# Edge counting in a graph network kernel: TensorE's register values are loaded behind the steps of the preceding epoch, ahead of the wait for the eviction

## What is computed

```python
aggr = jax.ops.segment_sum(x[src], dst, num_segments=x.shape[0])
h = aggr @ W_rel + b_rel + x @ W_root
...
agg = jax.ops.segment_sum(h[edge_src], edge_dst, num_segments=N) * inv_deg
return h @ W_self.T + agg @ W_neigh.T + b
```

## Time and profile before

| | us |
|---|---|
| median of 3 runs | 4267.49 |
| lowest and highest run | 4263.15, 4274.33 |
| span of the profiled execution | 4266.3 |
| TensorE matmuls busy in that span | 3043.3 |
| VectorE busy | 2017.8 |
| GpSimd busy | 2364.9 |
| ScalarE busy | 705.0 |

### The profile page before, as it was taken

How to read it: one execution, slowest core, us unless ns; L and a number is a source line. 1 busy time by engine, 2 the same in 40 slices (tenths; PEclk the granted TensorE clock), 3 DMA queues, 4 the chain that set the end, 5 groups by cost and what they waited for, 6 DMA issues and landing times.

```text
span 4266.3 us, 42581 instructions
## 1 busy us (share of the span) xinstructions
PE 3043.3 (71%) x12281; PEld 2000.6 (47%) x12281; DVE 2017.8 (47%) x4124; ACT 705.0 (17%) x1923; POOL 2364.9 (55%) x2466
## 2 busy tenths in 40 slices
PE   5666798996888888888376666666667666666666
PEld 3555454554666666565243333333344333433334
DVE  7777685467988888898631111111112111111112
ACT  2334201002444444343320000000001000000000
POOL 3000000004777777776237777777775777777776
PEclk8778898998999999899675555555557555555555
DMA  3544754463444444443041111111123111111112
GB/s 125 214 191 194 302 215 190 200 263 97 119 115 114 118 110 118 110 118 97 3 149 53 53 53 53 53 53 52 53 70 142 53 53 53 52 53 53 52 53 63
DMA packets 236740, 456.14 MB, mean 107 GB/s; under 512 B 64036, under 2 KB 183570, under 8 KB 231392
## 3 DMA queue, kind: packets, MB, share of 16 engines
q1 hardware_dynamic: 158728, 291.44, 18.8%
q0 software_dynamic: 77792, 161.98, 13.9%
HBM read 336.68 MB, written 116.51 MB: 106 GB/s over the span
## 4 chain that ended last, share of the span: by engine, by line
POOL 37%; PE 26%; issue 17%; DMA 15%; DVE 4%; ACT 2%; SPq 0%; ACTq 0%; DVEq 0%; POOLq 0%
POOL edge_buffers L574 21%; POOL round_buffers L1124 16%; DMA edge_buffers<-rel_table,relidx 13%; PE sums L794 9%; PE sums L602 4%; PE sums L706 3%; PE sums L702 3%; PE sums L1582 2%; PE sums L711 1%; ACT adj_window L737 0%; DMA adj<-adj_window 0%; ACT chunk_and_window L737 0%; DMA adj_chunk<-adj 0%; PE sums L1246 0%; DVE tile_moments L487 0%
## 5 line engine op out<-in xcount | busy, mean ns | idle before, releaser
L574 POOL DMA_INDIRECT edge_buffers<-rel_table,relidx x1612 | 1534.2, 952 | 586.0 <-PE sums L602 268.8
L602 PE MATMUL sums<-edge_buffers 128*128 128x128 f32 x3224 | 1254.7, 495 | 750.2 <-DMA edge_buffers<-rel_table,relidx 746.4
L602 PEld LDWEIGHTS sums<-edge_buffers 128*128 128x128 f32 x3224 | 802.1, 310 | 1206.0 <-issue 1205.1
L585 DVE TENSOR_SCALAR edge_buffers<-iota,rel 128x128 f32<-128x128 f32 x1612 | 335.2, 296 | 1644.4 <-PE sums L602 1644.4
L1124 POOL DMA_INDIRECT round_buffers<-xs_t,srcs x806 | 765.5, 950 | 570.9 <-DMA xd_t<-round_buffers 325.5
L631 ACT ACTIVATE trio<-sums,c_L_b 128x256 f32<-128x256 f32 (+1 forms) x16 | 8.0, 500 | 2020.4 <-PE sums L606 2020.4
L944 POOL IOTA trio<- 128x806 int32 x1 | 0.8, 805 | 603.8 <-ACT H L517 603.8
L1168 PE MATMUL sums<-round_buffers,ident 128*128 128x408 f32 x620 | 278.6, 533 | 27.6 <-DMA round_buffers<-xs_t,srcs 24.1
L1171 PEld LDWEIGHTS sums<-round_buffers 128*128 128x128 f32 x1612 | 243.5, 198 | 76.1 <-issue 65.6
L1268 ACT ACTIVATE trio<-sums 128x128 f32 x806 | 223.7, 278 | 279.7 <-PE sums L1246 196.7
L1171 PE MATMUL sums<-round_buffers 128*128 128x136 f32 x1612 | 244.8, 285 | 0.0
(11 more groups left out here) (289 smaller groups left out, 3000.0 us busy)
## 6 DMA issues: line engine op xcount, KB each, us to landing
chunk_and_window<-adj SPq DMA_DIRECT2D x10, 5600.0 KB, 15.8
round_buffers<-xd_t SPq DMA_DIRECT2D x806, 68.0 KB
adj_chunk<-adj SPq DMA_DIRECT2D x9, 5600.0 KB, 16.5
adj<-adj_window SPq DMA_DIRECT2D x11, 3850.0 KB, 11.5
adj<-chunk_and_window SPq DMA_DIRECT2D x10, 3850.0 KB, 11.3
edge_buffers<-rel_table,relidx POOLq DMA_INDIRECT x1612, 2.5
rel_table<-table_stages SPq DMA_DIRECT2D x50, 512.0 KB, 2.6
round_buffers<-xs_t,srcs POOLq DMA_INDIRECT x806, 2.5
```

What stands on the lines that cost most here:

```text
L574: nc.gpsimd.indirect_dma_start(slot(t), None, table[:, :], bass.IndirectOffsetOnAxis(ap=index[:, t:t + 1], axis=0)).then_inc(slot_sem(t), 16)
L585: made = nc.vector.tensor_scalar(round_hots(i)[:, k, :], iota[:, :], rel[:, t:t + 1], None, ALU.is_equal)
L602: nc.tensor.matmul(sums[:, bass.ds(place[k], P)], slot(t), round_hots(i)[:, k, :], start=False, stop=False).then_inc(summed_n, 1)
```

## The change

The register load of an epoch moves into a function of its own, `places_of_epoch`. The load of epoch 0 stands ahead of the loop. The load of epoch e + 1 is issued in epoch e, behind the 19 steps and ahead of the wait for the eviction of e - 1, the carry and the closing matmuls. The register of the carry of epoch e is kept in `carried` meanwhile. The last epoch loads nothing.

```diff
--- before.py
+++ after.py
@@ -687,15 +687,18 @@
                 if e == SHIFT_AT:
                     first_norm["shift"] = rows_shift(0, NT, (root_n, 1))
 
+        def places_of_epoch(e):
+            place = nc.values_load_multi_w_load_instructions(
+                steprow[0:1, e, 0:SLOTS], engines=(ENG.PE,), min_val=0, max_val=(SPANNED - 1) * CELLS,
+                skip_runtime_bounds_check_because="made on the chip from counts")[1]
+            return [nc.s_assert_within(v, 0, 2048 - CELLS, skip_runtime_bounds_check_because="made on the chip")
+                    for v in place[:STEPS_OF]] + [place[STEPS_OF]]
+
         def count_edges():
             T.need(stepped, A.now())
+            place = places_of_epoch(0)
             for e in range(EPOCHS):
                 half = sums[:, (e % 2) * 2048:(e % 2 + 1) * 2048]
-                place = nc.values_load_multi_w_load_instructions(
-                    steprow[0:1, e, 0:SLOTS], engines=(ENG.PE,), min_val=0, max_val=(SPANNED - 1) * CELLS,
-                    skip_runtime_bounds_check_because="made on the chip from counts")[1]
-                place = [nc.s_assert_within(v, 0, 2048 - CELLS, skip_runtime_bounds_check_because="made on the chip")
-                         for v in place[:STEPS_OF]] + [place[STEPS_OF]]
                 if e > 1:
                     nc.tensor.wait_ge(eout_n, e - 1)
                 for j in range(4):
@@ -706,10 +709,13 @@
                     m = nc.tensor.matmul(half[:, bass.ds(place[k], CELLS)], hot_lo[e % 2][:, :, k], hot_cell[e % 2][:, k, :],
                                          start=False, stop=False)
                 m.then_inc(estep_n, 1)
+                carried = place[STEPS_OF]
+                if e + 1 < EPOCHS:
+                    place = places_of_epoch(e + 1)
                 if e:
                     nc.tensor.wait_ge(eout_n, e)
                     nc.tensor.matmul(half[:, 0:CELLS], ident[:, :],
-                                     filled[(e - 1) // GROUP % 2][:, bass.ds(place[STEPS_OF], CELLS)],
+                                     filled[(e - 1) // GROUP % 2][:, bass.ds(carried, CELLS)],
                                      start=False, stop=False)
                 for j in range(4):
                     m = nc.tensor.matmul(half[:, j * 512:j * 512 + 1], zeros[:, 0:P], zeros[:, 0:1], start=False, stop=True)
```

## The result

The change makes the kernel slightly faster: 4249.91 us against 4264.31 us, medians of 7 runs each; the ratio is 0.996, 95% interval 0.9948 to 0.9972. Two of the changed kernel's seven runs, 4341.61 and 5059.26 us, had a lower granted clock and stay out of the ratio; the other five have a median of 4247.54. A second comparison (5 runs against 9) gave 4252.79 against 4267.24 us, ratio 0.9963 (0.9949 to 0.9976). That is 14.4 us, where 2.5 were forecast.

A forecast was written before the change was run, and what follows sets the result against it. TensorE's in-order sequencer, load plus 2.67 us per epoch, was taken as the bound of edge counting. 4266.3 − 4.0 (windows) + 1.5 (tail) = 4263.8, plus 1.2 from span to median: 4265 us; range 4249 to 4284.

The forecast's parts named there:

- rival A: Load after a window's store: escapes the packets, closing later or load's end unaffected; 4251 us, chance 0.17.
- TensorE's in-order sequencer is the bound, load plus 2.67: Edge counting: each epoch costs TensorE its register load plus 2.67 us of register operations and dispatch.
- (1): Wait for the eviction before the carry: already costs nothing, so the load placed ahead is worth 0 there.
- (2): Epoch without store packets: same sequencer work in another order, 1.36 + 2.67 us again, gain 0.
- (3): Window's fourth closing, eviction and store slip 1.50 us; stall moves from e = 29 to e = 30; 20 windows −4.0 us.
- the factor 2.22: Register load under store packets: each us of a quiet load falling there adds 2.22 us.
- an onset at 0.83: Register loads taken as slow from 0.83 us behind a store's issue, when packets begin; 0.66 us the earliest.
- (4): Tail: chunk loads and last store queue behind the store of w = 19, all slipping: +1.5 us.
- Rival B: Store's place: unchanged because closings aren't held up by the load; everything stays, 4267 us, chance 0.08.
- Rival C: VectorE's comparisons become late behind the 4.40 us stall and push the load of e = 33; 4283 us, chance 0.13.
- Rival D: Queue behind TensorE's sequencer full at twelve steps, about 0.6 us lost per window: +12, 4277 us, chance 0.07.

The follow-up runs named there:

- experiment 7: Kernel before with two register loads of 20 values per epoch, both in use: 5356.35 against 5222.78 us on the same chip, ratio 1.0246.
- experiment 2: Kernel before, TensorE untouched; SyncE holds each window's store until the next window's first epoch's steps are done: 4252.55 us, ratio 0.9963.

## Why the prediction was wrong

The forecast was "no change", 4265 us; the kernel came out 0.4% faster, clear of noise, at the low edge of its range (4249 to 4284) and near the 4251 us of rival A. The mechanism was the forecast one, and one term was mis-sized.

- *"TensorE's in-order sequencer is the bound, load plus 2.67":* right. Doubling the loads added 140 us of them and 134 us to the time (experiment 7), and the rest of an epoch is 2.63 us on the mean.
- *(1) The eviction wait gains no cover:* right. L717 waits for nothing of ScalarE's.
- *(2) A quiet epoch is worth 0:* right, 4.02 and 4.19 us in the shown window against 4.02 and 4.18.
- *(3) The store slips by 1.50 us against the loads:* right in kind, 4.17 − 2.62 = 1.55. **The step that failed** is the length of the load that ends under the store, "2.12 us on the mean": measured 1.51. By the factor 2.22 that is an overlap with the slow time of 0.07 us, where 0.34 were forecast. Two sizes were off. The load starts 0.28 us ahead of the store on the mean of the 20 windows, not 0.19. And the packets' start was taken as the moment from which a load is slow:

```profile
GB/s 0 0 0 0 0 0 0 0 0 0 0 0 0 0 0 0 0 0 0 0 0 0 0 0 0 0 0 3080 4107 3080 3080 2053 1027 0 0 0 0 0 0 0
```

This is the stretch 200.39 to 201.59 of the changed kernel in 40 slices; packets begin in slice 27, 0.81 us behind the issue, as in the earlier trace rows. The load from 200.24 would have ended quietly 1.21 us behind the issue and took 0.38 us more, which at 2.22 us per us is 0.17 us of overlap: slow from 1.04 us on. The load of the next window starts 0.29 us ahead of its store and takes 1.53: 1.07 − 0.17 / 2.22 = 0.99. All 20 windows agree: the six loads whose quiet end would lie at most 1.00 us behind the issue take 1.36 us, and the 14 with a quiet end at 1.03 to 1.21 take 1.42 to 1.74, which by the factor 2.22 is slow from 0.98 to 1.05. So the onset is 1.0 us behind the issue, 0.17 us later than I had it. Together 0.26 us less overlap, times 2.22, is 0.58 us a window, 12 us over 20. The factor 2.22 turned a quarter of a microsecond into all of the 12 us between the forecast gain of 2.5 and the measured 14.4. The 0.699 us of SyncE's load, which I took as support for an onset at 0.83, does not carry over: begun at 0.79 it would have ended quietly at 1.06, and from 1.0 on the factor 2.22 makes that 0.40 us. Its 0.699 would need an onset at 0.87. So one load of another engine, of a single register, was a poor measure of TensorE's; why it was slowed more stays open.
- *(4) The tail, +1.5:* right as to the whole. The store of a window slips by 1.5 us against the stage (the first is issued 0.3 us later though the first fill was 1.2 us earlier, 66.79 against 67.96). The loads give 20 x 0.79 = 15.8 us, the last store is issued 15.76 us earlier, and 14.4 are left at the end. Of the 1.4 us given back 0.5 are in the last store, 20.33 us from issue to landing instead of 19.83, and 0.3 between there and the last eviction of the round at 623.47; the other 0.6 come behind it and can't be told from noise.
- *Rival A* named this outcome, at 0.17, with 4251 us; it took the escape for a case of its own and not for the far end of a steep term. Whole escapes came only in the six windows above. *Rival B* falls: the store is issued 4.17 us behind the start of the load, not 2.62.
- *Rival C* (comparisons late) did not come: in the timeline VectorE starts L677 at 213.06, 4.01 us behind the end of the 4.38 us load, where 4.25 was feared, and is done 7.6 us behind it, before it is wanted at 8.1.
- *Rival D* (a full queue) was right in kind and far too high in its price. The register operations of e = 30, up to 211.5 us and up to 211.56, and the first step:

```profile
L709 PEldq FUSED_REGOPS  x18: 37/37/42, 209.3 to 211.3; - x18
...
L709 PEldq FUSED_REGOPS  x19: 37/37/42, 209.3 to 211.6; - x19
...
L709 PE MATMUL sums<-trio x1: 292/292/292, 211.5 to 211.5; 128*128 128x100 f16 x1
```

Eighteen operations went out 0.115 to 0.145 us apart, the last of them at 211.28; the nineteenth came at 211.55, 0.27 us behind it and 0.02 us behind the start of the first step. In 16 of the 20 windows behind epoch 3 the nineteenth comes at those 0.02 us, and in no epoch is the sequencer more than 18 steps ahead. So it stops there, at half as many again as the twelve of the earlier trace rows (other epochs of the kernel before reach 14). The rest of the epoch e = 30 and its like is 2.61 us on the mean instead of 2.53 (2.53 also in experiment 2, with the old order and the same loads), which is 0.08 us a window, 1.6 us over 20, where 12 were priced. The Trainium skill ("TensorE: Matmul & The Clock Gate", table at the head) gives a depth of 64, by which the prediction had 19 steps with their weight loads, 38, fit. The trace does not bear that count out: the sequencer was held at 18 steps, 36 by the same count. What else takes up the queue stays open.

The range fitted the uncertainty, 4251 and 4249 at its low end against medians of 4247.54 to 4252.79, the lowest of them just outside. What was wrong was to call the middle of a steep, unshown term likely enough for a forecast of "same".

## What to carry to other kernels

A stall whose releaser is "issue" may be a register load, and a register load's length may depend on what the DMA does at that moment: look at its longest rows, not at the median (here 4.4 us against 1.36). A move on one engine that seems neutral shifts all that it releases; here the worth of the change was where a store fell between loads, and a wait on SyncE gave the same. Cutting the store to fit between the loads gave over four times as much. Where a cost is a product of an overlap and a steep factor, measure the edge before trusting a sum to a few microseconds.

## What was not expected of the hardware

- A load of 20 registers on TensorE takes 1.36 us with no packets in flight and 4.4 us under a store, 68 and 220 ns a register. It need not be a store to `adj`: in the kernel before the load of epoch 0 takes 3.35 us at 64.55, 20 us ahead of the first store, while the DMA engines are busy for 0.91 of that stretch (326 GB/s). The Trainium skill ("Runtime: NRT & Kernel Launch", instruction fetch mechanics) gives some 200 ns per register; this case shows that only under DMA traffic.
- The slow time of TensorE's load begins 1.0 us behind the store's issue in all windows of the changed kernel that show an onset, some 0.2 us behind the first packet (0.81). Why not with the packet stays open.
- TensorE's sequencer was never more than 18 register-addressed steps ahead of the first one running.
- A register load whose values nothing uses was not in the program that ran, so a cost can't be doubled by repeating it without use.
